# Softplus in two halves, with its bias copies on DVE, in a transformer and Mamba kernel on one core

## The reference, cut to what matters

```python
xs, z = jnp.split(h @ in_w, 2, axis=-1)
xs = silu(xs)
proj = xs @ xproj_w
dt = softplus(proj[..., :512] + dt_bias)
Bm, Cm = proj[..., 512:576], proj[..., 576:]
# step: hst = hst * exp(dt * A) + (dt * x) * B ;  y = sum over the 64 states of hst * C
```

## Time and profile before

| | us |
|---|---|
| median of 3 runs | 3404.33 |
| lowest to highest | 3403.07 to 3409.16 |
| profiled execution, whole | 3408.53 |
| its span in the trace | 3406.7 |

### The profile page before, as it was taken

The page is one execution under the profiler, slowest core; times in us unless marked ns, Lnnn a source line. Parts: engine busy times, 40 slices in busy tenths (PEclk is TensorE's granted clock), DMA queues, the critical chain, the costliest instruction groups (busy, mean ns, idle before and its releaser), DMA issues.

```text
span 3406.7 us, 69419 instructions
## 1 busy us (share of the span) xinstructions
PE 3024.2 (89%) x21944; PEld 2683.9 (79%) x21944; DVE 2909.5 (85%) x3331; ACT 2989.0 (88%) x6469; POOL 2945.7 (86%) x1552
## 2 busy tenths in 40 slices
PE   8778898999988999899988999899998899998776
PEld 6568787888878888788877888788887888887765
DVE  3269998899888998889988999889988899899885
ACT  1189999899989999899999999899998999999994
POOL 0069998999888998889988998889988899899995
PEclk6689999999989999899999999899998999999998
DMA  4011111111111111111111111112111111111210
GB/s 174 0 42 43 48 45 47 42 51 48 43 48 47 47 47 42 49 45 48 45 47 43 49 48 43 48 41 52 48 43 46 48 47 46 42 45 45 54 47 26
DMA packets 163033, 162.50 MB, mean 48 GB/s; under 512 B 17610, under 2 KB 156874, under 8 KB 162644
## 3 DMA queue, kind: packets, MB, share of 16 engines
q1 hardware_dynamic: 162644, 157.69, 17.2%
HBM read 154.44 MB, written 3.18 MB: 46 GB/s over the span
## 4 chain that ended last, share of the span: by engine, by line
PE 45%; POOL 16%; ACT 15%; issue 13%; DVE 9%; DMA 1%; DVEq 1%; POOLq 0%; ACTq 0%; SPq 0%
POOL hst L408 12%; PE ps L1225 12%; PE ps L1241 11%; ACT dA L567 7%; PE ps L993 6%; ACT uBT L553 4%; DVE hst L892 4%; PE ps L1002 4%; POOL uBT L417 4%; PE ps L1065 3%; PE ps L1040 2%; PE ps L1114 1%; PE ps L1049 1%; PE ps L1233 1%; PE ps L1150 1%
## 5 line engine op out<-in xcount | busy, mean ns | idle before, releaser
L408 POOL TENSOR_TENSOR hst<-hst,C_sb 128x1024 f32<-128x1024 f32 x1024 | 2441.0, 2409 | 232.8 <-DVE hst L892 226.6
L892 DVE TENSOR_TENSOR_SCAN hst<-dA,ps 128x512 f32<-128x512 f32 x2048 | 2384.0, 1205 | 177.6 <-PE ps L1241 160.1
L567 ACT ACTIVATE dA<-dt,A 128x255 f32<-128x255 f32 x4096 | 1758.5, 504 | 2.8 <-DVE hst L892 2.7
L1225 PE MATMUL ps<-ident,uBT 128*128 128x128 f32 x8192 | 1288.2, 281 | 134.0 <-DVE hst L892 103.0
L1241 PE MATMUL ps<-ident,hst 128*128 128x128 f32 x8192 | 1267.9, 278 | 104.5 <-POOL hst L408 103.7
L1225 PEld LDWEIGHTS ps<-ident,uBT 128*128 128x128 f32 x8192 | 994.2, 145 | 299.0 <-DVE hst L892 152.5
L553 ACT ACTIVATE uBT<-uT,BT 128x512 f32<-128x512 f32 x1536 | 1052.2, 720 | 130.9 <-PE ps L1225 120.0
L1241 PEld LDWEIGHTS ps<-ident,hst 128*128 128x128 f32 x8192 | 979.6, 144 | 139.8 <-POOL hst L408 139.7
L417 POOL TENSOR_TENSOR uBT<-uT,BT 128x512 f32<-128x512 f32 x512 | 559.3, 1092 | 185.3 <-DVE uT L829 185.3
L476 ACT ACTIVATE probs<-ps,nmax 128x128 f32<-128x128 f32 (+1 forms) x256 | 93.9, 423 | 101.6 <-DVE nmax L764 100.7
L993 PE MATMUL ps<-xsT,w_xp 128*128 128x256 f32 x512 | 130.6, 380 | 0.0
(11 more groups left out here) (142 smaller groups left out, 2110.7 us busy)
## 6 DMA issues: line engine op xcount, KB each, us to landing
C_sb<-c_dram SPq DMA_DIRECT2D x1024, 128.0 KB, 2.9
gate_l<-gate_rows_dram SPq DMA_DIRECT2D x16, 256.0 KB, 3.7
x_att<-in_x_dram SPq DMA_DIRECT2D x8, 256.0 KB, 3.0
w<-in_L_cond_W_dram SPq DMA_DIRECT2D x2, 1024.0 KB
out_dram<-x_glu SPq DMA_DIRECT2D x8, 256.0 KB, 3.2
wg<-in_L_cond_mlp_w_dram SPq DMA_DIRECT2D x3, 512.0 KB, 11.4
w_xp<-_L_cond_fwd_xproj_w_dram SPq DMA_DIRECT2D x1, 1280.0 KB, 12.4
w_xp<-_L_cond_bwd_xproj_w_dram SPq DMA_DIRECT2D x1, 1280.0 KB, 15.0
```

Source lines behind the costliest of these rows:

```text
L408: pool.tensor_tensor(h, h, C_sb[:, n % FED:n % FED + 1, :].to_broadcast([P, KI, NB]), ALU.mult).then_inc(hC_ready.sem, 1)
L567: done = act.activation(dA[:, n % NT, c, lo:hi], dt[:, d, c, lo:hi], ACT.Exp, scale=A[:, d, c, n:n + 1])
L892: dve.tensor_tensor_scan(pair(hst[:, n % NR]), pair(dA[:, n % NT]), ps[:, BANK_U + (2 * n + e) % (2 * NU), :][:, way], 0.0, ALU.mult, ALU. ...
L1225: last = pe.transpose(ps[:, BANK_U + (2 * n + e) % (2 * NU), o:o + P], uBT[:, n % NF, j, c * P:(c + 1) * P], ident[:, :])
```

## The change

ACT no longer reads the products. DVE adds the bias in one operation for each block and writes x to `pre`. From there ACT takes abs, exp, 1 + e and log for blocks 0 and 1, then for blocks 2 and 3, and DVE's four operations come twice as well, at half the size; the relu is folded into the second of them as a maximum with 0. PE transposes u in two halves, each into a bank of its own, and DVE copies each. The stage has 27 steps for 24, with other rooms, so every other step of the plan moves too.

```diff
-    STEPS = dict(norm=6, qkv=11, heads=37, proj=5, up=12, down=10, ins=12, dts=24, post=10, glu=17)
+    STEPS = dict(norm=6, qkv=11, heads=37, proj=5, up=12, down=10, ins=12, dts=27, post=10, glu=17)
...
-                ins=[HEAVY] * 8 + [LIGHT, LIGHT, LONG, LIGHT], dts=[HEAVY] * 12 + [LIGHT] * 2 + [HEAVY] * 3 + [LONG] + [HEAVY] * 4 + [LIGHT] * 2,
+                ins=[HEAVY] * 8 + [LIGHT, LIGHT, LONG, LIGHT], dts=[HEAVY] * 23 + [LIGHT, HEAVY, HEAVY, LIGHT],
...
-                    + stage("own", "dts", 0, 2) + meanwhile(stage("own", "dts", 2, 14), stage("last", "norm", 0, 4))
-                    + meanwhile(stage("own", "dts", 14, 21), stage("last", "norm", 4, 6))
-                    + stage("own", "dts", 21, STEPS["dts"]) + stage("last", "glu") + first)
+                    + stage("own", "dts", 0, 2) + meanwhile(stage("own", "dts", 2, 13), stage("last", "norm", 0, 4))
+                    + meanwhile(stage("own", "dts", 13, 22), stage("last", "norm", 4, 6))
+                    + stage("own", "dts", 22, STEPS["dts"]) + stage("last", "glu") + first)
...
+        half = lambda t, h: t[:, 2 * h:2 * h + 2, :]
...
-                    if i % 2 == 1 and 7 <= i < 7 + 2 * KI:
-                        m = (i - 7) // 2
-                        act.wait_ge(dt_mm.sem, dt_mm.at(p, m + 1))
-                        act.activation(expo[:, m, :], ps[:, BANK_P + m % 2, 0:NB], ACT.Abs, bias=dtb_col[:, d, m:m + 1])
-                        act.activation(pre[:, m, :], ps[:, BANK_P + m % 2, 0:NB], ACT.Relu,
-                                       bias=dtb_col[:, d, m:m + 1]).then_inc(pre_ready.sem, 1)
-                    if i == 15:
-                        act.wait_ge(pre_ready.sem, pre_ready.at(p, KI))
-                        act.activation(expo, expo, ACT.Exp, scale=-1.0).then_inc(exp_ready.sem, 1)
...
+                    for h in range(2):
+                        e_h, w_h = half(expo, h), half(channels(uT[:, d]), h)
+                        if i == 10 + 4 * h:
+                            act.wait_ge(pre_ready.sem, pre_ready.at(p, 2 * h + 2))
+                            act.activation(e_h, half(pre, h), ACT.Abs).then_inc(abs_ready.sem, 1)
+                        if i == 11 + 4 * h:
+                            act.wait_ge(abs_ready.sem, abs_ready.at(p, h + 1))
+                            act.activation(e_h, e_h, ACT.Exp, scale=-1.0).then_inc(exp_ready.sem, 1)
+                        if i == 12 + 4 * h:
+                            act.wait_ge(exp_ready.sem, exp_ready.at(p, h + 1))
+                            act.activation(w_h, e_h, ACT.Identity, bias=ones_col[:, 0:1]).then_inc(one_ready.sem, 1)
+                        if i == 13 + 4 * h:
+                            act.wait_ge(one_ready.sem, one_ready.at(p, h + 1))
+                            act.activation(half(dt[:, d], h), w_h, ACT.Ln).then_inc(log_ready.sem, 1)
...
+                    if i % 2 == 0 and 6 <= i < 6 + 2 * KI:
+                        m = (i - 6) // 2
+                        dve.wait_ge(dt_mm.sem, dt_mm.at(p, m + 1))
+                        dve.tensor_scalar(pre[:, m, :], ps[:, BANK_P + m % 2, 0:NB], dtb_col[:, d, m:m + 1], None, ALU.add).then_inc(pre_ready.sem, 1)
+                    for h in range(2):
+                        x_h, e_h, dt_h = half(pre, h), half(expo, h), half(dt[:, d], h)
+                        if i == 14 + 4 * h:
+                            dve.wait_ge(one_ready.sem, one_ready.at(p, h + 1))
+                            dve.scalar_tensor_tensor(e_h, half(channels(uT[:, d]), h), -1.0, e_h, ALU.add, ALU.subtract).then_inc(corr_ready.sem, 1)
+                        if i == 15 + 4 * h:
+                            dve.wait_ge(corr_ready.sem, corr_ready.at(p, h + 1))
+                            dve.scalar_tensor_tensor(x_h, x_h, 0.0, e_h, ALU.max, ALU.subtract).then_inc(sum_ready.sem, 1)
+                        if i == 16 + 4 * h:
+                            dve.wait_ge(sum_ready.sem, sum_ready.at(p, h + 1))
+                            dve.wait_ge(log_ready.sem, log_ready.at(p, h + 1))
+                            dve.tensor_tensor(dt_h, dt_h, x_h, ALU.add).then_inc(dt_ready.sem, 1)
+                        if i == 17 + 4 * h:
+                            dve.wait_ge(dt_ready.sem, dt_ready.at(p, h + 1))
+                            dve.wait_ge(in_ready.sem, in_ready.at(p, 1))
+                            dve.tensor_tensor(x_h, dt_h, half(xsT, h), ALU.mult).then_inc(u_ready.sem, 1)
+                        if i == 24 + h:
+                            dve.wait_ge(uT_mm.sem, uT_mm.at(p, h + 1))
+                            dve.tensor_copy(uT[:, d].rearrange("p (j n) -> p j n", n=DI)[:, :, h * NB:(h + 1) * NB],
+                                            ps[:, BANK_P + h, :].rearrange("p (j n) -> p j n", n=NB)).then_inc(uT_ready.sem, 1)
...
+                    if i in (22, 23):
+                        h = i - 22
+                        pe.wait_ge(u_ready.sem, u_ready.at(p, h + 1))
+                        for j in range(TT):
+                            for c in range(2):
+                                last = pe.transpose(ps[:, BANK_P + h, j * NB + c * P:j * NB + (c + 1) * P], pre[:, 2 * h + c, j * P:(j + 1) * P], ident[:, :])
+                        last.then_inc(uT_mm.sem, 1)
+                    if i == 26:
+                        pe.wait_ge(uT_ready.sem, uT_ready.at(p, 2))
```

More of the change, by code:

```diff
@@ L547, in forcing @@
                 if n == 0:
-                    act.wait_ge(uT_ready.sem, uT_ready.at(p, 1))
+                    act.wait_ge(uT_ready.sem, uT_ready.at(p, 2))
                     act.wait_ge(BT_ready.sem, BT_ready.at(p, 1))
@@ L560, in decays @@
                 if n == 0 and e == 0:
-                    act.wait_ge(dt_ready.sem, dt_ready.at(p, 1))
+                    act.wait_ge(dt_ready.sem, dt_ready.at(p, 2))
                 if r_known(p, n) >= NT:
@@ L1145, in prepare @@
                             last.then_inc(dt_mm.sem, 1)
-                    if i == 21:
-                        pe.wait_ge(u_ready.sem, u_ready.at(p, 1))
+                    if i in (22, 23):
+                        h = i - 22
+                        pe.wait_ge(u_ready.sem, u_ready.at(p, h + 1))
                         for j in range(TT):
-                            for c in range(KI):
-                                last = pe.transpose(ps[:, BANK_P + j, c * P:(c + 1) * P], pre[:, c, j * P:(j + 1) * P], ident[:, :])
+                            for c in range(2):
+                                last = pe.transpose(ps[:, BANK_P + h, j * NB + c * P:j * NB + (c + 1) * P], pre[:, 2 * h + c, j * P:(j + 1) * P], ident[:, :])
                         last.then_inc(uT_mm.sem, 1)
-                    if i == 23:
-                        pe.wait_ge(uT_ready.sem, uT_ready.at(p, 1))
+                    if i == 26:
+                        pe.wait_ge(uT_ready.sem, uT_ready.at(p, 2))
                     yield
@@ L1286, in before @@
                             pe.wait_ge(pre_ready.sem, pre_ready.at(p + 1, KI))
-                        if plan.steps[j] == ("own", "dts", 21) and has_prev:
+                        if plan.steps[j] == ("own", "dts", 22) and has_prev:
                             pe.wait_ge(hT_ready[LN_GLU].sem, hT_ready[LN_GLU].at(b - 1, 1))
```

34 lines of the change are left out of this document (6 added, 28 removed).

## The result

| | us |
|---|---|
| before, median of 4 runs | 3404.14 (3403.07 to 3409.16) |
| changed, median of 4 runs | 3451.97 (3451.18 to 3455.55) |
| ratio | 1.014, 95% interval 1.0122 to 1.0157 |
| profiled execution of the changed kernel, its span | 3455.55, 3453.7 |

The changed kernel is slower by 48 us. The forecast was 3426 (+22) with a range of 3377 to 3448: the side was right, the size was a little under half of what came, and the time lies 4 us outside the range. It lies midway between rivals C (3447) and D (3457).

What follows compares the result with a forecast made beforehand. It followed DVE, whose lateness in POOL's starved parts is the program's. Six steady forward passes +3, seven backward +25, first chain -4, last forward pass's chain -1.5: together +22 on a 3404.3 us median, so 3426, range 3377 to 3448.

Steps and rivals of the forecast that it cites:

- rivals C: Plan: squeezing the stages ahead saves nothing, since waits from engine to engine hold them, not work; 3447 us, chance 0.10.
- rival D: Softplus chain: the change doesn't take DVE's wait for ACT away; 3457 us, chance 0.03.
- The stall: Softplus chain, line 815: DVE's wait for ACT, 3.25 us forward and 1.70 backward, goes.
- The exclusion: Halved chain: DVE operations with two SBUF inputs and POOL's block each other; four 1.2 us waits, net +3.7 forward, +3.0 backward.
- The bias copies: End of dt products: DVE's copies wait for PE's products and delay scans, 1.3 us a forward pass, 2.4 a backward one.
- rival B: dt products: the copies delay nothing, since DVE finds each product done; about 3401 us, chance 0.18.
- The prologue: Chain ahead of the first pass, last product to first use of uT: 11.5 us falls to 7.4, so -4.
- The plan: Stages ahead lose halves but keep their work, saving 1.2 us a forward pass and 3.45 a backward one.
- the squeeze: Three more steps raise the sum of rooms from 147 to 155; each half lost elsewhere saves 0.87 to 1.45 us.
- backward passes over 5 us longer: Sign set for the rival in which lost halves save nothing; the forecast itself had backward passes some 3 us longer.
- Rival A: Softplus chain: DVE's wait for ACT goes and DVE-POOL blocking doesn't grow, halves meeting POOL's pauses; some 3383 us, chance 0.22.

Runs made afterwards that it cites:

- e13: e8 with 1 + e, the corrected value and the sum kept in PSUM, all arithmetic kept: 3359.82 us, ratio 0.9855 to the kernel before.
- e3: Changed kernel, but ACT makes abs and relu of the products from PSUM again, without DVE's bias copies: 3434.36 us, ratio 1.0084 to the kernel before.
- e2: Changed operations on the kernel before's plan of 24 steps: 3404.01 us, ratio 1.0006 to the kernel before.
- e7: e2 with ACT making abs and relu of the products, without DVE's bias copies: 3409.37 us, ratio 1.0011 to the kernel before.
- e1: Operations of the kernel before on the changed kernel's plan of 27 steps: 3428.08 us, ratio 1.0072 to the kernel before.
- e4: Kernel before with only the bias copies moved to DVE, chain whole, old plan: 3399.20 us, ratio 0.9977 to the kernel before.
- e8: Changed kernel with its stage's 27 rooms summing to 44, so all other stages stand in their old halves: 3409.01 us, ratio 1.0008 to the kernel before.
- e5: Changed kernel with each chain's eight two-input DVE operations replaced by same-size copies from PSUM, arithmetic left out: 3378.86 us, ratio 0.9924 to the kernel before.
- e12: Changed kernel with e8's rooms and e5's copies from PSUM together, arithmetic left out: 3346.31 us, ratio 0.9829 to the kernel before.
- e6: e2 with DVE's two-input operations grouped as dependent pairs behind scans of second halves: 3471.82 us, ratio 1.0185 to the kernel before.
- e10: e2 with DVE's two-input operations paired behind scans of second halves, each pair from different chain halves, independent: 3427.71 us, ratio 1.0076 to the kernel before.

## Why the prediction went wrong, step by step

**The stall: right.** DVE no longer waits for ACT in a chain. With it rival D is out, though its 3457 lies as near to the measured time as C's 3447.

**The exclusion: right in kind and size.** The forecast was four waits of 1.2 us in each of 13 chains, 62 us, and 43 net of what the kernel before paid. Four operations in each chain are slow, and DVE's time beyond that of free ones rises from 28.4 to 76.8 us, by 48. Taking the exclusion away gave 73 us on the new plan and (1.0008 - 0.9829) x 3404 = 61 on the old rooms, both with the chains of the first and last passes and with whatever the clock gives back. The slow operations take 0.66 and 1.73 us by turns, and the POOL operations that meet one 0.36 to 0.44 us more (2.73 for 2.37, 1.48 for 1.04), not 0.6. The Trainium skill (SBUF — State Buffer, "Who interferes with whom") states that a DVE instruction with at most one SBUF input doesn't contend with GpSimd, outside the perf modes in which DVE uses two ports. e13's rows agree, 0.66 to 0.70 us in the middle of a POOL operation against 1.73.

**The bias copies: right behind the backward products, wrong ahead of the forward chain.** The forecast was +2.4 and +1.3 a pass. With e3 beside it, the changed kernel loses 2.7 us in halves 96 to 128 of a backward pass and nothing in halves 0 to 64 of a forward one. And it loses them only on the new plan. There the last product and its copy share half 105, as the prediction saw, and the wait is 1.87. Where the copy comes a half later (forward passes, and every pass of e2 against e7) it costs nothing, as rival B said. So the term of 6 x 1.3 was wrong, and the one of 7 x 2.4 was of the right size but belonged to the plan's rounding and not to the copies alone.

**The prologue: right.** From the last copy out of a dt product to the first use of uT it takes 186.77 - 178.80 = 8.0 us for 11.5, so -3.5 for the forecast -4. The other 3.9 us of the -7.4 lie ahead of that, and so does e1's lead of 3.6, whose operations are those of before; their cause stays open. The halves did it and not the copies: in e4 the same stretch takes 190.98 - 178.78 = 12.2.

**The plan: the step that failed.** The prediction priced the squeeze as lost halves, each saving 0.87 to 1.45 us, together 31 us. It took every half that a stage loses as time saved, and put the waits that closer steps make from engine to engine at nothing. e1 shows +24 us for the plan without the copies. In their place the runs show 3.0 us lost in halves 64 to 80 of a forward pass (1.3 of waits and 1.7 of TensorE's lower clock) and 2.8 ahead of half 96 of a backward one. The sum held only part of the error, because another term erred the other way: without its squeeze the forecast says 22 + 31 = 53 us for the operations on the old rooms, and e8 took 0.0008 x 3404 = 3 us more than before. About 25 us of these 50 are the copies' terms (6 x 1.3 + 7 x 2.4), which cost nothing there, and 3 lie ahead of the first scan. Some 20 us, chiefly in the backward chain (e8's halves 96 to 128 take 1.0 more than before, where the forecast without squeeze and copies has 3.6 + 3.45 - 2.4 = 4.7), I can't assign to one term. That the side came out right and the size within a factor of about two is luck in part: two large errors of opposite sign stand behind it.

The mechanism of the plan term is that of rival C, which had a chance of 0.10: what lies ahead is held by waits from engine to engine. Its sign, backward passes over 5 us longer, came true (5.4). C was too mild all the same, since it let the squeeze save nothing and the runs show that it costs. Its sum was too small too: it took back 2.0 of the 3.45 us a backward pass, and the whole would have given 22 + 31 = +53. Neither C nor any other rival had a term for the clock. A plan that spreads steps evenly and rounds to whole halves puts two dependent steps behind one half at some places, and then a wait between PE and DVE stands ahead of a force or a scan. That the plan costs 24 us, and 45 together with the copies, is shown by e1 and e8. That the collisions at halves 71 and 84 are what costs is read from the traces at those places; no single pair was moved by itself, and the clock was separated from the waits only in the forward passes.

**Rival A** named the right prize (e5 and e12 are faster than before), but not the way: pauses of POOL don't save the halves from it, only another home for one input does.

## What to carry to other kernels

Where a planner spreads side work over a loop, a stage with more steps moves every other stage: compare which dependent steps share a slot before and after, look at TensorE's granted clock behind every new idle time of PE, keep the stage's total room, and time the new plan with the old operations. Count the DVE operations with two SBUF inputs beside POOL's work, since splitting one in two nearly doubled the number of waits here (31 in e4, 59 in e2); put one input into PSUM where a bank is free rather than search for a better place.

## What the runs showed of the hardware that I had not expected

POOL gets in between two DVE operations that both need what it needs, even if they are independent and issued back to back: 0.67 us for the first, 2.74 and 2.85 for the second (e6, e10), with a POOL product in between (2.73 in e6). In e6 this befalls 22 of 32 operations of line 826 and 30 of 32 of line 834, and grouping is worse than spreading (3471.82 us against 3404.01 for the same operations spread). And an operation whose output lies in PSUM as well as one input is as fast as one in SBUF, 0.68 to 0.70 us for 128x512 (e13).

TensorE's granted clock fell to its lower level for 3.4 us behind idle times of PE of 0.84 and 1.31 us in one half, in each steady forward pass of the changed kernel. The four matmuls of a force then took 1.06 us for 0.60, and the stretch of 16 halves 1.7 us longer than with the same waits at full clock.
